# Token rows and means turned to channel-major ahead of the quads of half 0, in place; VectorE adds them to half 0's sums

## The reference

```python
x = x + conv(_ln_c(x))                    # conv(v) = v + filtered v
t = _to_tokens(x)                         # (8, 1024, 64)
probs = softmax(logits); top_probs, top_idx = top_k(probs, 2)
hidden = silu(x @ w1[e]) * (x @ w2[e]);   out = hidden @ w3[e]
t = t + sum over the 2 chosen of 16 experts of weight * out
x = _from_tokens(t, x)                    # back to channels x pixels
```

## Time and profile before

| what | value |
|---|---|
| time, median of 3 runs | 330.17 us (330.09 to 330.7) |
| the profiled execution | 331.79 us, span 330.0 us |
| TensorE busy in the span | 254.0 us (77%) |
| VectorE busy | 237.4 us (72%) |
| ScalarE busy | 185.5 us (56%) |
| GpSimd busy | 96.4 us (29%) |
| TensorE's mean granted clock | 0.88 of 2.4 GHz |

### The profile page before, as it was taken

How to read it: one execution, slowest core, us unless ns; L and a number is a source line. 1 busy time by engine, 2 the same in 40 slices (tenths; PEclk the granted TensorE clock), 3 DMA queues, 4 the chain that set the end, 5 groups by cost and what they waited for, 6 DMA issues and landing times.

```text
span 330.0 us, 7880 instructions
## 1 busy us (share of the span) xinstructions
PE 254.0 (77%) x2569; PEld 211.4 (64%) x2569; DVE 237.4 (72%) x664; ACT 185.5 (56%) x439; POOL 96.4 (29%) x93
## 2 busy tenths in 40 slices
PE   1949966575883774388999999888996989864884
PEld 1935644475822563257888989777985878753663
DVE  1792558557979999789988885875667566615984
ACT  3759883466402897213787887334465455424763
POOL 2005336424101577000333323024321210007850
PEclk9985999777565599599999999997699999995999
DMA  7999333333100233703485564767766552323551
GB/s 210 361 222 313 125 120 121 121 123 123 45 0 2 80 110 117 142 0 81 109 167 119 132 159 117 109 132 157 138 128 137 134 122 64 84 66 102 169 148 64
DMA packets 63522, 41.03 MB, mean 124 GB/s; under 512 B 51834, under 2 KB 58340, under 8 KB 62844
## 3 DMA queue, kind: packets, MB, share of 16 engines
q1 hardware_dynamic: 60156, 30.02, 37.0%
q0 software_dynamic: 3168, 10.50, 10.2%
q10 hardware_dynamic: 160, 0.01, 0.0%
HBM read 14.31 MB, written 19.95 MB: 104 GB/s over the span
## 4 chain that ended last, share of the span: by engine, by line
PE 48%; DVE 27%; issue 8%; ACT 7%; DMA 6%; POOL 1%; DVEq 1%; ACTq 0%; POOLq 0%; SPq 0%
PE banks L972 15%; PE banks L959 8%; PE banks L960 7%; DVE tok L1264 4%; DMA xs<-sorted_y,back 4%; PE banks L990 3%; PE banks L886 3%; DVE xs L1351 3%; PE banks L769 2%; DVE tok L1261 2%; PE banks L982 2%; DVE ct L1055 2%; PE banks L894 2%; DVE xs L1344 1%; PE banks L707 1%
## 5 line engine op out<-in xcount | busy, mean ns | idle before, releaser
L1448 POOL DMA_INDIRECT sorted_x<-xs,addr x32 | 34.5, 1079 | 86.7 <-ACT xs L614 85.8
L1454 POOL DMA_INDIRECT xs<-sorted_y,back x32 | 32.7, 1023 | 81.4 <-DMA sorted_y<-filt 47.1
L972 PE MATMUL banks<-w_all,power 128*125 x388 | 53.6, 282 | 2.0 <-DVE block_end L1237 0.7
L1340 DVE SCALAR_TENSOR_TENSOR power<-banks,fold 128x500 f32<-128x500 f32 (+1 forms) x50 | 33.0, 660 | 29.4 <-ACT fold L634 25.5
L972 PEld LDWEIGHTS banks<-w_all,power 128*125 128x125 f32 x388 | 47.6, 194 | 5.6 <-issue 4.3
L649 ACT CAST xs<-xs 64x320 f16<-64x320 f32 x64 | 29.2, 456 | 37.4 <-DVE xs L1344 19.9
L614 ACT CAST xs<-banks 128x384 f16<-128x384 f32 x64 | 28.1, 469 | 18.4 <-PE banks L886 18.3
L634 ACT ACTIVATE fold<-banks 128x500 f32<-128x500 f32 (+1 forms) x50 | 28.8, 575 | 17.2 <-PE banks L960 14.9
L1330 DVE COPY work<-w_all 128x256 uint16 x194 | 30.8, 223 | 7.7 <-issue 7.4
L886 PE MATMUL banks<-shared,tok 128*64 128x131 f16 x320 | 24.4, 268 | 11.4 <-DVE tok L1264 9.7
L1264 DVE SCALAR_TENSOR_TENSOR tok<-perm,local,tok 128x320 f16<-128x320 f16 x64 | 32.2, 542 | 0.0
(11 more groups left out here) (189 smaller groups left out, 521.2 us busy)
## 6 DMA issues: line engine op xcount, KB each, us to landing
sorted_x<-zeros SPq DMA_DIRECT2D x2, 3125.0 KB
sorted_y<-filt SPq DMA_DIRECT2D x24, 125.0 KB
sorted_y<-enh SPq DMA_DIRECT2D x24, 125.0 KB
w_raw<-in_L_ffn_w SPq DMA_DIRECT2D x5, 512.0 KB, 16.5
xs<-in_x SPq DMA_DIRECT2D x8, 256.0 KB, 5.1
out<-cen_sq SPq DMA_DIRECT2D x8, 256.0 KB, 2.2
shared<-in_t_fwd SPq DMA_DIRECT2D x1, 1024.0 KB, 7.8
shared<-in_t_neg SPq DMA_DIRECT2D x1, 1024.0 KB, 11.7
```

Of the source, the lines that this page charges most:

```text
L972: last = nc.tensor.matmul(y_bank(q)[0:BW, b * C:(b + 1) * C], hid[:, q % RING, b * BW:(b + 1) * BW], of_expert(experts[(q % NQ % 2) * QUAD ...
L1340: nc.vector.scalar_tensor_tensor(hid[:, q % RING, 0:w], bank[2 + q % 2][:, 0:w], HSCALE / WSCALE, gated[:, q % 2, 0:w], ALU.mult, ALU.mult ...
L1448: nc.gpsimd.indirect_dma_start(out=sorted_x[k].rearrange("(g s) c -> g (s c)", s=GRP), out_offset=bass.IndirectOffsetOnAxis(ap=addr[:, k, ...
L1454: nc.gpsimd.indirect_dma_start(out=yl[m % YL_RING].rearrange("g s c -> g (s c)"), out_offset=None, in_=sorted_y[k].rearrange("(g s) c -> g ...
```

## The change

The residual is taken out of the sums of each pair. A block of 512 pixels is turned at once: TensorE's `turn_residual(n)` does the same two kinds of products for four pairs into bank 7, in the order of the image, and ScalarE's `residual_out(n)` copies the bank back over the same rows of `ct`, which then is channel-major. Four blocks (0 to 3) are turned between half 0's sort and `counts_for(1)`, the other four one each in quads 0 to 3, ahead of `down`. As there is one bank, each turn waits for the copy before it (`turn_done`).

For half 0 (blocks 0 to 3) the sums start with the one-hot products, and VectorE's `early_result(n)` adds the bank and the rows of `ct` into `res`. For half 1 (blocks 4 to 7) the sums start with one fp32 product of identity and 512 columns of `ct`, and ScalarE copies the result, now without a change of order, since all sums are written in the order of the image. TensorE and SyncE wait for `res_early` or `res_done` as the block asks. `turn_later` also waits for all turns, which use the same bank.

```diff
--- before.py
+++ after.py
@@ -84,6 +84,8 @@
 ACC_BANKS = (4, 5)
 RET_START, RET_STEPS, BACK_LAG = 2, 18, 2
 RESULT_LAG = 3
+TURN_BANK, GAP_TURNS = 7, 4
+EARLY = NBLK // HALVES
 STORE_AFTER = {9: 0, 13: 1, 17: 2}
 SLOT_GROUPS = SLOT_BLOCKS * GBLK
 EXPERT = 4 * HID + 2 * C
@@ -333,7 +335,8 @@
         y_stored = [sem(f"y_stored{r}") for r in range(YS_RING)]
         gathered = [sem(f"gathered{r}") for r in range(YL_RING)]
         parts_zero, yw_done, yhi_done, ylo_done, back_ps = (sem(n) for n in ("parts_zero", "yw_done", "yhi_done", "ylo_done", "back_ps"))
-        res_done = sem("res_done")
+        res_done, res_early = sem("res_done"), sem("res_early")
+        turn_ps, turn_done = sem("turn_ps"), sem("turn_done")
         stored = [sem(f"stored{r}") for r in range(2)]
 
         x_v = x.rearrange("(g h) c a b -> (h c) g (a b)", h=2)
@@ -393,6 +396,14 @@
         def misc_of(k):
 
             return bank[MISC_BANK] if k == 0 else bank[Y_BANK][:, BLK // 2:]
+
+        def result_taken(engine, n):
+
+            engine.wait_ge(*((res_early, n + 1) if n < EARLY else (res_done, n + 1 - EARLY)))
+
+        def in_image(t, u):
+
+            return t.rearrange("p (k x q y) -> p k q x y", k=KT, q=2, y=16)[:, u // 2, u % 2, :, :]
 
         def rows_in(a):
 
@@ -441,7 +452,7 @@
                 sp.dma_start(gate_raw[h * C:(h + 1) * C, :], gate_w).then_inc(in_gate, 16)
             sp.dma_start(gate_b_all[:, :], gate_b.rearrange("(o e) -> o e", o=1).to_broadcast([P, E])).then_inc(in_gate, 16)
             def store(n):
-                sp.wait_ge(res_done, n + 1)
+                result_taken(sp, n)
                 sp.dma_start(out_v[:, n // 2, (n % 2) * BLK:(n % 2 + 1) * BLK], res[:, n % 2, :]).then_inc(stored[n % 2], 16)
 
             sp.wait_ge(zeros_set, 1)
@@ -652,14 +663,20 @@
                 act.wait_ge(back_ps, BP * (n + 1))
                 if n >= 2:
                     act.wait_ge(stored[n % 2], 16 * (n // 2))
-                nc.scalar.copy(res[:, n % 2, :].rearrange("p (k x q y) -> p k q x y", k=KT, q=2, y=16),
-                               bank[ACC_BANKS[n % 2]].rearrange("p (k q x y) -> p k q x y", k=KT, q=2, y=16)).then_inc(res_done, 1)
+                nc.scalar.copy(res[:, n % 2, :], bank[ACC_BANKS[n % 2]]).then_inc(res_done, 1)
 
             def results_by(m):
 
-                if m >= BP + RESULT_LAG - 1 and (m - RESULT_LAG + 1) % BP == 0:
+                if m >= BP * (EARLY + 1) + RESULT_LAG - 1 and (m - RESULT_LAG + 1) % BP == 0:
                     result((m - RESULT_LAG + 1) // BP - 1)
 
+            def residual_out(n):
+
+                act.wait_ge(turn_ps, n + 1)
+                nc.scalar.copy(ct[:, BP * n:BP * (n + 1), 0:P], bank[TURN_BANK].rearrange("p (j i) -> p j i", j=BP)).then_inc(turn_done, 1)
+
+            for n in range(GAP_TURNS):
+                residual_out(n)
             gap_exponential(1)
             load_table(ACT.Silu)
             for q in range(HALVES * NQ + 1):
@@ -673,12 +690,13 @@
                     sorted_out(n, 0)
                 for before in downs_in(q):
                     y_out(before)
+                if GAP_TURNS + q < NBLK:
+                    residual_out(GAP_TURNS + q)
                 for n in sorts_in(q):
                     sorted_out(n, 1)
                 if k == 1:
                     for m in pairs_in(i, RET_START, RET_STEPS):
                         high_part(m)
-                        results_by(m)
             for m in range(HP, HALVES * HP):
                 high_part(m)
                 results_by(m)
@@ -905,6 +923,7 @@
             def turn_later(n):
 
                 pe.wait_ge(hott_done, n)
+                pe.wait_ge(turn_done, NBLK)
                 turn_hots(n, bank[XT_BANK])
 
             pe.wait_ge(id16_set, 2)
@@ -976,23 +995,37 @@
             def back_to_tokens(m):
 
                 n, u = m // BP, m % BP
-                sums = bank[ACC_BANKS[n % 2]][:, u * P:(u + 1) * P]
+                acc = bank[ACC_BANKS[n % 2]]
                 if u == 0 and n >= 2:
-                    pe.wait_ge(res_done, n - 1)
-                nc.tensor.matmul(sums, ct[:, m, 0:P], ident, start=True, stop=False)
-                for h in range(2):
-                    nc.tensor.matmul(sums[h * C:(h + 1) * C, :], both_parts[:, 2 * m + h:2 * m + h + 1].to_broadcast([P, C]), mean_rows[:, :],
-                                     start=False, stop=False)
+                    result_taken(pe, n - 2)
+                if u == 0 and n >= EARLY:
+                    pe.wait_ge(turn_done, n + 1)
+                    nc.tensor.matmul(acc, ident, ct[:, BP * n:BP * (n + 1), 0:P], start=True, stop=False)
                 pe.wait_ge(hott_done, m + 1)
                 pe.wait_ge(ylo_done, 2 * (m + 1))
                 for s in range(GRP):
                     for a in range(2):
-                        last = nc.tensor.matmul(sums, y_parts[m % SPLIT_RING][:, s, a, :, :], hott[m][:, s, :], start=False, stop=(s == GRP - 1 and a == 1))
+                        last = nc.tensor.matmul(in_image(acc, u), y_parts[m % SPLIT_RING][:, s, a, :, :], hott[m][:, s, :].rearrange("g (x y) -> g x y", y=16),
+                                                start=(n < EARLY and s == a == 0), stop=(s == GRP - 1 and a == 1 and (n < EARLY or u == BP - 1)))
                 last.then_inc(back_ps, 1)
 
+            def turn_residual(n):
+
+                pe.wait_ge(turn_done, n)
+                for u in range(BP):
+                    m = BP * n + u
+                    sums = in_image(bank[TURN_BANK], u)
+                    nc.tensor.matmul(sums, ct[:, m, 0:P], ident, start=True, stop=False)
+                    for h in range(2):
+                        last = nc.tensor.matmul(sums[h * C:(h + 1) * C], both_parts[:, 2 * m + h:2 * m + h + 1].to_broadcast([P, C]), mean_rows[:, :],
+                                                start=False, stop=True)
+                last.then_inc(turn_ps, 1)
+
             pe.wait_ge(mean_rows_done, 2)
+            pe.wait_ge(hott_done, HP)
+            for n in range(GAP_TURNS):
+                turn_residual(n)
             pe.wait_ge(wsplit, 3)
-            pe.wait_ge(hott_done, HP)
             counts_for(1)
             for q in range(HALVES * NQ + 1):
                 k, i = q // NQ, q % NQ
@@ -1010,6 +1043,8 @@
                 if q >= 1:
                     for t in sorts_in(q - 1):
                         turn_later(t)
+                if GAP_TURNS + q < NBLK:
+                    turn_residual(GAP_TURNS + q)
                 for t in sorts_in(q):
                     sort_pair(t, 0)
                 for before in downs_in(q):
@@ -1350,10 +1385,22 @@
                     of_tile = y_parts[m % SPLIT_RING][tile_half(h), :, :, h, :]
                     nc.vector.tensor_tensor(of_tile[:, :, 1, :], yl[m % YL_RING][tile_half(h), :, :], of_tile[:, :, 0, :], ALU.subtract).then_inc(ylo_done, 1)
 
+            def early_result(n):
+
+                dve.wait_ge(back_ps, BP * (n + 1))
+                dve.wait_ge(turn_done, n + 1)
+                if n >= 2:
+                    dve.wait_ge(stored[n % 2], 16 * (n // 2))
+                nc.vector.tensor_tensor(res[:, n % 2, :].rearrange("p (j i) -> p j i", j=BP), bank[ACC_BANKS[n % 2]].rearrange("p (j i) -> p j i", j=BP),
+                                        ct[:, BP * n:BP * (n + 1), 0:P], ALU.add).then_inc(res_early, 1)
+
             def return_step(m):
                 weigh(m)
                 if m >= 1:
                     low_part(m - 1)
+                n, after = divmod(m - RESULT_LAG + 1, BP)
+                if after == 0 and 1 <= n <= EARLY:
+                    early_result(n - 1)
 
             for i in range(FETCH_AHEAD):
                 fetch(i)
```

## The result

The changed kernel takes **346.1 us** on the median (342.95 to 350.26, 4 runs) against 330.4 beside it: a ratio of 1.042, 95% interval 1.030 to 1.054, slower. The forecast was 343.7, range 335 to 347.5. The profiled execution took 344.77, with a span of 342.9 (before 330.0).

What follows compares the result with a forecast made beforehand. Bounds: VectorE's routing in the gap, then TensorE in quads 4 to 24, a VectorE-ScalarE ring in half 1's quads, VectorE in the tail. 17.0 - 3.8 + 0.3 = +13.5 on 330.2 gives 343.7 us, range 335 to 347.5.

Steps and rivals of the forecast that it cites:

- The gap: TensorE's wait for half 1's routing, 128.7 to 137.6: four turns don't fit, making the counts 8.7 us late.
- busy 2.45 of 4.4 us, less than in either row. I take the half clock: From sort's end to second turn, TensorE's busy share was taken as too low for the full clock; turns 4.59 us apart.
- the clock stays up: Rival: full clock in the gap, turns ending 4.1 us late, quad 4 10.5 late; 337.2 us in all; chance 0.22.
- A pair at 0.58: In the turns, one pair's residual, two fp32 and two fp16 matmuls, takes 0.58 us at the full clock.
- Quads 0 to 3: One turn in each quad, hidden only in TensorE's 1.5 us of idle time: these quads grow by 8.6 us.
- Half 1's quads: Where half 0's sums return, 227 to 290: two holdups go and three result copies leave ScalarE; -3.8 us.
- the copies: Half 1's quads: three of four result copies leave ScalarE's path between high part and gate, 0.49 us each, 1.4 in all.
- The ring: Half 1's quads: VectorE and ScalarE set the pace (product, fetch, weigh, high part, gate), 3.28 us a round, without TensorE.
- 1.72 - 0.75 = 1.0: Half 1's quads: the product at 237.31 waits for TensorE; without residuals its wait becomes normal, saving 1.0 us.
- 2.12 - 0.75 = 1.4: Half 1's quads: the product at 257.84 waits for TensorE; without residuals its wait becomes normal, saving 1.4 us.
- slow again later: Rival: TensorE, with less to do in half 1's quads, falls to half clock once or twice more; 347.7 us; chance 0.10.
- Tail: After half 1's quads: the fourth early result adds 0.2 us on VectorE, TensorE may run at half clock; +0.3 in all.

Runs made afterwards that it cites:

- two banks: The changed kernel with the gap's four turns alternating between two PSUM banks; 342.2 us against 330.5.
- rows in idle time: The kernel before with only half 0's rows turned, two turns while TensorE waits for the sort, two in the gap, VectorE taking half 0's results; 329.6 us against 332.4.
- filled: The changed kernel with three unused 16-bit matmuls of 512 columns behind each of the gap's first three turns; 343.2 us against 330.5.
- half 0's turns alone: The changed kernel without turns in quads 0 to 3, half 1's residual pair by pair as before the change; 341.3 us against 330.5.
- no turns: The changed kernel without its eight turns and their copies, output incomplete; 331.7 us against 330.5.
- rows only: The changed kernel with two banks for the gap's turns and the mean's products left out; 331.7 us against 332.4, one profiled run.
- means last: The changed kernel with two banks, each turn doing all four pairs' rows first, then the mean's eight products; 334.3 us against 330.8, one profiled run.
- VectorE's copies alone: The kernel before the change with half 0's four results copied from PSUM by VectorE instead of ScalarE; 330.5 us against 332.4.
- the fourth copy alone: The kernel before the change with only half 0's fourth result, in the tail, copied by VectorE; 331.3 us against 330.8, one profiled run.
- mean-stays: The changed kernel with the mean's two products per pair put back ahead of the returned sums, turns of rows only; 331.8 us against 330.8.

## Why the prediction came out right, and which step was wrong

**The gap: size right, reason wrong.** Turns 4.59 apart were forecast, 4.64 measured; counts 8.7 late, 9.0 counted from R; a pair at the half clock 0.93, 0.97. The step that fails is "busy 2.45 of 4.4 us, less than in either row. I take the half clock". With two banks TensorE was busy throughout and got half the clock; with the mean elsewhere it was busy 4.81 of 8.90 and got all of it. The busy share between turns isn't what decides. (By the prediction's own terms the busy time in that stretch is 2.32, not 2.45; it makes no difference.) The forecast read the right level from a rule that the runs refute, and that is luck. What stands in the turn matters: in the four kernels in which rows and means alternate the clock fell within 1.7 us of the first turn's start, and in two banks it stayed at half through 12.60 us without idle time; in four of the five with rows alone or the means last it held through the turns. But it doesn't decide alone: in the run with rows in idle time it fell with rows alone in the turn, and in the filled run alternating turns held the full clock once fillers had brought it back. Why the clock falls stays open. The rival "the clock stays up" was out for the change as it is; with the mean left with the sums it would have been right for the gap.

**A pair at 0.58: taken as given.** The earlier trace rows show it, with weight loads of 0.30 and 0.11, and the prediction multiplied it by 32 (the pairs of all eight turns) without asking what it is made of. It is 0.24 of rows and 0.35 that grouping cuts to 0.12. The Trainium skill has a rule for this that the prediction didn't weigh: "TensorEngine Tiling (Array Packing)", section "Key Properties", says that a change between tilings drains TensorE. The mean's products use 64 of the 128 columns and the rows' all, so a pair has two such changes; grouped, a turn has two instead of eight. The runs are in line with it: if the drain is all that grouping saves, it is (4 x 0.59 - 1.44) / 6, an estimate of 0.15 us for each. The same edit also takes away changes between fp32 and 16-bit products, and with them places where an fp32 weight load (0.30 for two) isn't covered; no run here tells these apart.

**Quads 0 to 3: right, 1.1 too high.** +8.6 forecast, +7.5 measured, and the run with half 0's turns alone shows 7.3 for the four turns there. That TensorE-bound quads give nothing back was right: quad 5 to quad 28 takes 65.5 us before and after.

**Half 1's quads: the copies right, the holdups not.** -3.8 forecast, -1.7 measured, and -1.5 to -2.5 in the five runs with the same half 1 but other turns (no turns, two banks, filled, rows only, means last). The ring and the copies were right (early results fit, by 0.03 at 261.92), though smaller: 0.8 with VectorE's copies alone instead of 1.4. The term "1.72 - 0.75 = 1.0" isn't shown to be the residual's. Of the 1.7, 1.3 lie between quad 28 and weigh 4 (18.7 before, 17.4 after), where before had the half clock and after didn't; the run with the fourth copy alone, which changes nothing there, had the full clock and 17.3. The term that fails is "2.12 - 0.75 = 1.4", which blamed the long holdup on the residual. The rows above show what it is: VectorE does two products 1.13 apart (265.62, 266.75; before the change 251.70 and 252.84), so the low part between them and the next comes late, at 268.64, and TensorE's sums, behind which the next up stands, wait for its end:

```profile
269.63 0.72 PE L1008 MATMUL banks<-scratch,xs 128*128 128x128 f16 x10 [2.40 <-DVE xs L1386]
```

Before, the low part ended at 255.71 and the sums started at 256.00, so the residual cost 0.29 there, not 1.4; and the half clock, which came at 270.3, took that back. The rival "slow again later" came true in part as well: the clock was at half from 270.3 to 273.7 and from 284.0 to 287.4, which it wasn't before between 240 and 298. It wasn't an alternative to the likeliest case but an addition, in some executions.

**Tail: wrong sign.** +0.3 forecast, -1.1 measured. The early result does take the 0.52 that VectorE waited behind pair 18 for its own 0.69, and the 512-column product hides; but the wait of 1.19 at pair 30, which the prediction had no row for, is gone. It is -0.9 to -1.1 in every run with all of the change's half 1.

Measured less forecast is +0.3 in the gap, -0.8 in quads 0 to 3 (with the 0.3 that was to come back behind them), +2.1 in half 1's quads and -1.4 in the tail. That these all but cancel is luck too; 343.7 is 1.1 from the profiled execution and 2.4 from the median.

## What to carry to other kernels

Before you multiply a row's duration, ask what it is made of and what stands next to what: here more than half of a pair's 0.59 us went when its two smallest products were left out, and their order mattered more than place, banks or waits. Before moving work into an engine's idle time, measure the same products alone and grouped; here that decided between 4% slower and 1% faster. Most of a slowdown of 4% came from two products of 0.04 us each (eight take 0.35 when grouped), in the wrong place. And a stage's gain in one execution can be the clock's: look for a run in which that stage was left as it was.

## What the hardware showed that was not expected

- TensorE's clock can stay at half while it is never idle: fp32 rows and 64-column 16-bit means alternating, 12.60 of 12.60 us busy, granted 0.50; the same products grouped, 4.90 of 4.90 busy, granted 1.00. "TensorE: Matmul & The Clock Gate" of the Trainium skill, section "Why this matters for your kernels", ties the fall to idle gaps between matmul bursts. In the two-bank run the idle time just ahead of the turns was 1.17 us, the same as in the rows-only and mean-stays runs, which kept the clock; so an idle gap doesn't tell these runs apart.
- TensorE's load of the experts' numbers into registers varies, in 26 loads of the changed kernel (min, median, max in ns):

```profile
L941 PEldq TENSOR_LOAD <-owner x26: 319/809/2558, 124.4 to 301.1; - x26
```

  The longest starts at 266.7; the kernel before has one of 2.36 us at 252.8. Both stand beside the start of half 0's first output store (266.2 and 252.3). Here the wait for the low part covers them nearly to the end. That the store is the cause was not tried.
